# Gated heads: the value products move from the end of a slot to directly behind the scores

## What is computed

```python
def _L1_ffn_ref(x, w_q, w_k, w_gate, value_experts, output_experts):   # x already normalised
    HEADS, DIM_HEAD, EXPERTS = (8, 64, 8)
    gates = jax.nn.sigmoid((x @ w_gate).reshape(b, n, HEADS, EXPERTS).transpose(0, 2, 1, 3))
    sel = jnp.argmax(gates, axis=-1)
    gm = jax.nn.one_hot(sel, EXPERTS, dtype=x.dtype) * gates
    values = jnp.einsum('bhne,ehdk,bnd->bhnk', gm, value_experts, x)
    sim = jnp.einsum('bhid,bhjd->bhij', q * SCALE, k)
    sim = jnp.where(causal_mask, jnp.finfo(sim.dtype).min, sim)
    attn = jax.nn.softmax(sim, axis=-1)
    out = jnp.einsum('bhij,bhjk->bhik', attn, values)
    out = jnp.einsum('bhne,ehkd,bhnk->bhnd', gm, output_experts, out)
    return out.sum(axis=1)
...
    x = x + _L1_ffn_ref(_layernorm(x, axis=-1), ...)
```

## Time and profile before

| quantity | value |
|---|---|
| median of 3 runs | 3820.56 us (3817.29 to 3824.1) |
| the profiled execution, its own time | 3820.83 us |
| its span in the trace | 3819.1 us |
| PE busy (TensorE matmul) | 3505.7 us, 92% |
| DVE busy (VectorE) | 2801.9 us, 73% |
| ACT busy (ScalarE) | 2065.1 us, 54% |

### The profile page before, as it was taken

How to read it: one execution, slowest core, us unless ns; L and a number is a source line. 1 busy time by engine, 2 the same in 40 slices (tenths; PEclk the granted TensorE clock), 3 DMA queues, 4 the chain that set the end, 5 groups by cost and what they waited for, 6 DMA issues and landing times. The chain is left out here.

```text
span 3819.1 us, 91322 instructions
## 1 busy us (share of the span) xinstructions
PE 3505.7 (92%) x28322; PEld 2917.3 (76%) x28322; DVE 2801.9 (73%) x8965; ACT 2065.1 (54%) x6485; POOL 395.4 (10%) x582
## 2 busy tenths in 40 slices
PE   6999999899999999339968889999799999999999
PEld 5888888688888888239956656676588888888887
DVE  5666666677777776646658877888788878788786
ACT  5777777677777776325545548888432223222232
POOL 0000000000000000341168302222000000000000
PEclk9999999999999999669989999999899999999999
DMA  3000000010000000542211000000200000000000
GB/s 101 1 0 0 0 0 0 18 51 11 11 11 13 14 11 1 175 137 77 78 55 45 15 17 20 22 22 17 87 26 11 14 8 16 8 11 14 8 14 9
DMA packets 56108, 109.69 MB, mean 29 GB/s; under 512 B 8368, under 2 KB 27184, under 8 KB 55728
## 3 DMA queue, kind: packets, MB, share of 16 engines
q1 hardware_dynamic: 46656, 80.72, 6.7%
q0 software_dynamic: 8464, 26.22, 2.1%
q10 hardware_dynamic: 864, 1.19, 0.1%
HBM read 72.46 MB, written 35.65 MB: 28 GB/s over the span
## 5 line engine op out<-in xcount | busy, mean ns | idle before, releaser
L2255 DVE TENSOR_TENSOR f_zgT<-f_zT,f_ps_g 128x512 fp32r<-128x512 f32 x512 | 327.3, 681 | 14.0 <-PE f_ps_g L2086 9.9
L639 ACT ACTIVATE c_pr<-c_sm,c_nmx 128x256 f32<-128x256 f32 x512 | 254.5, 498 | 147.7 <-DVE c_nmx L485 147.7
L127 PE MATMUL f_ps_out<-f_out_rounded,f_zgT 128*128 128x256 f32 x1024 | 295.3, 288 | 0.0
L128 PE MATMUL f_ps_out<-f_out_rest,f_zgT 128*128 128x256 f32 x1024 | 289.5, 283 | 0.0
L2208 DVE TENSOR_TENSOR f_gv<-f_ps_v,f_gm 128x512 f32<-128x512 f32 x256 | 175.6, 686 | 154.2 <-PE f_ps_v L129 154.1
L129 PE MATMUL f_ps_out<-f_out_rounded,f_zgT 128*128 128x256 f32 x1024 | 288.0, 281 | 0.0
L639 ACT ACTIVATE a_pr<-a_sm,a_nmx 128x128 f32<-128x128 f32 (+1 forms) x512 | 227.1, 445 | 98.1 <-DVE a_nmx L485 98.1
L485 DVE CUSTOM_DVE_ANT_0 a_sm<-a_ps_s,causal 128x128 f32<-128x128 f32 (+1 forms) x512 | 152.5, 354 | 156.8 <-PE a_ps_s L371 156.7
L485 DVE CUSTOM_DVE_ANT_0 c_sm<-c_ps_s,c_mask 128x256 f32<-128x256 f32 x512 | 186.7, 420 | 87.1 <-PE c_ps_s L371 86.7
L127 PE MATMUL f_ps_v<-f_val_rounded,f_xs 128*128 128x512 f32 x512 | 214.8, 419 | 6.7 <-DVE f_gv L2208 6.7
L2337 ACT ACTIVATE f_pr<-f_sm,f_nmx 128x128 f32<-128x128 f32 (+1 forms) x256 | 115.0, 450 | 185.5 <-DVE f_nmx L2228 185.5
(11 more groups left out here) (384 smaller groups left out, 11231.8 us busy)
## 6 DMA issues: line engine op xcount, KB each, us to landing
f_slot_rows<-f_run POOLq DMA_DIRECT2D x1, 9216.0 KB, 34.8
f_rows<-f_slot_rows SPq DMA_DIRECT2D x72, 128.0 KB, 2.0
f_slot_out<-f_y SPq DMA_DIRECT2D x72, 128.0 KB, 1.9
c_ctx_stage<-in_ctxT SPq DMA_DIRECT2D x32, 256.0 KB, 2.8
small<-in_f_w SPq DMA_DIRECT2D x16, 512.0 KB, 3.9
x_sb<-in_x SPq DMA_DIRECT2D x8, 512.0 KB, 8.3
small<-in_c_w SPq DMA_DIRECT2D x8, 512.0 KB, 4.0
c_mask_stage<-in_mask SPq DMA_DIRECT2D x16, 256.0 KB, 3.0
```

The lines of the kernel that those rows point to most:

```text
L127: nc.tensor.matmul(out, sh, mh, start=start, stop=False, **kw)
L128: nc.tensor.matmul(out, sh, ml, start=False, stop=False, **kw)
L639: last = nc.scalar.activation(pr[:, r, i, 0:n], sm[:, j, i, 0:n], ACT.Exp, bias=nmx[:, j, i:i + 1], scale=-1.0, accum_out=sums[:, r, i:i + 1])
L2255: last = nc.vector.tensor_tensor(zgT[:, k % 2, r], zT[:, s % 2, r, :].bitcast(F32).unsqueeze(1).broadcast_to([P, 2, S]), ps_g[:].rearrange ...
```

## The change

The call of `values` moves, with its condition, from behind the four rounds (and behind `turn_x`) into round k = 1, directly behind `scores` and ahead of `turn`. It is the same call with the same waits inside. Nothing is changed on VectorE, ScalarE, GpSimd or the DMA queues.

```diff
@@ -2114,6 +2114,8 @@
                         project_v(now[0], s, k, b)
                     if k == 1 and ahead:
                         scores(ahead[0], ahead[1], now[0] + 1 if now else ahead[0] + 1)
+                    if k == 1 and (at := lagged(b, s, 3, STEPS)):
+                        values(at[0], at[1])
                     if k % 2 and two:
                         turn(two[0], two[1], k // 2, two[2])
                     if four:
@@ -2122,8 +2124,6 @@
                             output(four[0], four[1], k - 1, four[2])
                 if s == STEPS - 1 and (not isinstance(b, int) or b + 1 < B):
                     turn_x(b + 1)
-                if at := lagged(b, s, 3, STEPS):
-                    values(at[0], at[1])
                 if four:
                     output(four[0], four[1], K - 1, four[2])
                 if now and s == STEPS - 1:
```

## The result

The changed kernel takes 3852.84 us (median of 6 runs), the kernel before 3820.51 us in the same comparison: a ratio of 1.0082, with a 95% interval of 1.0071 to 1.0093. It is slower by 32 us; the forecast was 3852. The profiled execution of the changed kernel took 3850.67 us.

The account below looks back on a forecast made before the run. VectorE's chain from gate_v(2) to output(3) was taken as the bound, with busy TensorE merely covering its wait. Terms 29.2 + 1.65 + 2.7 - 1.9 = 31.7 us on 3820.83 gave 3852 us, range 3834 to 3868.

Parts of the forecast that it names:

- The price of the step: values between scores and turn on TensorE: delays everything behind it, project_v(2) included, by 0.80 us a slot.
- Neither bound: Limits on the cost of values at its new place: 0.47 us at least, 0.96 us at most.
- The chain from gate_v(2) to output(3): VectorE's unbroken 4.33 us from gate_v(2) to gate_z(3), whose start releases output(3) 1.32 us later; it passes on the delay.
- The slack of 0.10: VectorE's time to spare before output(3) in s = 1 and 2: 0.10 us, taken off the 0.80 us delay.
- The batch: Growth of a regular batch: 0.60 + 0.70 + 0.70 + 0.25 = 2.25 us; thirteen batches give 29.2 us.
- The end: Last batch, without turn_x, 2.7 us longer; three emptying slots gain 1.9 us as values hides in waits.
- The beginning: Batch 1 grows 1.65 us; slot 3 adds 0, and slot 4 adds 0 because its 2.11 us stall absorbs values.
- the faster one: Rival: TensorE's own stream decides, so 0.18 us a slot is gained, 3810 us; chance 6%.
- Full price: Rival: no slack counts, neither VectorE's nor turn_x; 45.3 us more, 3866 us; chance 10%.
- cheap neighbour: Rival: values costs less behind scores, 0.63 or 0.47 us, because its drain merges; 3842 or 3834 us; chance 8%.
- nothing: Rival: the delay is caught up elsewhere, as in slot 4, and time stays at 3821 us; chance 3%.
- the clock: Rival: TensorE's idle time at slot ends lowers the granted clock; some 60 us more, beyond 3900; chance 2%.

Follow-up runs that it names:

- e2: Changed kernel with VectorE's norm of the first head (0.78 us) moved from round 2 to the end of round 3: 0.9989 of the kernel before.
- e3: Changed kernel plus an unused second copy of the four products of values at the old place in s = 0, 1, 2: 1.0092 of the kernel before.
- e6: Changed kernel plus the same extra products as e3, but directly behind values at the new place, ahead of project_v(2): 1.0171 of the kernel before.
- e4: Changed kernel with e2's edit, gate_z(3) ahead of gate_v(3) on VectorE and spread_one(3) ahead of the second turn on TensorE: 0.9957 of the kernel before.
- e5: Kernel before, values at its old place, with the same cuts to VectorE's path as e4: 0.9999 of the kernel before.
- e1: Changed kernel with values in round 2, directly behind project_v(2), instead of behind scores: 1.0031 of the kernel before.
- e7: e4 without its edit on TensorE, so turn stays ahead of spread_one(3): 0.9987 of the kernel before.
- e8: e4 with scores and values in s = 1 to 3 behind spread_one(0), ahead of project_v(1): 0.9970 of the kernel before.

## Why the prediction was right, step by step

**The price of the step, 0.80 us**: right, 0.81 at the new place (3056.58 to 3057.39), with the idle times of 0.33 and 0.17 that I had taken over from the neighbours. Neither bound, 0.47 or 0.96, was near.

**The chain from gate_v(2) to output(3)**: right, 4.33 us and 1.33 us, and e2, e3 and e6 show that it is the cause. The slack of 0.10, read from a slot that truly waits, was right too: slots with s = 1 or 2 could have grown by 0.80 without it, and a batch would be 0.2 longer.

**The batch**: 2.25 us forecast, 2.26 measured between neighbouring batches. Slot by slot, from one output(3) to the next, the growth is 0.59 us in s = 0 (17.84 to 18.43), 0.69 in s = 1, 0.71 in s = 2 and 0.27 in s = 3 (17.05 to 17.32), where I had 0.60, 0.70, 0.70 and 0.25. So the parts are right, not only the sum. The 13 batches run between these additions to x_sum, before and then after (timeline of DVE):

```profile
2822.16 0.69 DVE L2263 TENSOR_TENSOR f_x_sum<-f_x_sum,f_ps_out 128x512 f32<-128x512 f32 x1 [0.97 <-PE f_ps_out L129]
...
3708.00 0.69 DVE L2263 TENSOR_TENSOR f_x_sum<-f_x_sum,f_ps_out 128x512 f32<-128x512 f32 x1 [1.08 <-PE f_ps_out L129]
```
```profile
2821.42 0.69 DVE L2263 TENSOR_TENSOR f_x_sum<-f_x_sum,f_ps_out 128x512 f32<-128x512 f32 x1 [0.43 <-PE f_ps_out L129]
...
3736.92 0.69 DVE L2263 TENSOR_TENSOR f_x_sum<-f_x_sum,f_ps_out 128x512 f32<-128x512 f32 x1 [0.54 <-PE f_ps_out L129]
```

885.84 us became 915.50: 29.7 more, where the sum had 29.2.

**The end** (last batch and emptying slots): 0.8 forecast; the last addition to x_sum starts at 3815.99 before and 3845.82 after, so from the rows above 107.99 became 108.90, 0.9.

**The beginning**: the one part that was mis-sized, by 1.3 of the 31.7 us. From the stage's first transposes (2698.56 before, 2697.50 after) to the first row above it is 123.60 before and 123.92 after: +0.3, where the sum had 1.65. Slots by the first load of project: slots 5 to 7 grew by 1.68, as forecast, and slot 3 is 12.78 us in both (the zero is right). Slot 4 is the term that failed: not zero, but 0.70 shorter (2750.80 to 2771.54 before, 2749.08 to 2769.12 after). Up to spread_one(1) it is 8.78 us in both, so values does vanish in that wait; what is gained lies behind it (last section). The remaining 0.66 us were gained in slots 0 and 1, before values runs for the first time, so the change didn't make them: in the ten traces slot 0 takes anything from 14.3 to 16.4 us, and in the kernel before it is at the top of that.

**The total**: in the profiled executions the difference is 29.8 us (29.7 + 0.9 + 0.3, less 1.1 for an earlier start of the stage); that of the medians is 32.3. The spread of single runs, 8 us for the kernel before, is wider than that gap, so the close agreement of 3852 with the median owes something to luck, and the batch is the better witness.

**What I said the profile would show**: idle time ahead of gate_v(2) of 1.3 us (measured 1.21: 0.27 and 0.94); output(3) waiting about 0.9 in s = 0, 1 and 2 (0.83 or 0.84), 0.4 in s = 3 (0.43), near 50 us in total (44.7). Scores to turn came to 1.66, as forecast (1.65).

**The rivals**: the faster one (TensorE decides) is false for this kernel, but its price was real. e4 against e5 gives 0.82 us a batch for the new place, 0.2 a slot, where I had 0.18. The rule of the Trainium skill (TensorEngine Tiling (Array Packing), Key Properties), that a change of tiling mode drains TensorE, is in line with this: one change less in a slot, and 0.2 us less. It only decides once TensorE is the bound. Full price is excluded by s = 3 (0.27 us, not 0.80), cheap neighbour by the 0.81 us of the step, nothing by the 2.26 us of every batch, and the clock by its 1.00 in the batches.

## What to carry to other kernels

An engine that is busy all the time isn't therefore the bound at every point: look for a wait of almost no idle time that recurs in nearly every round (0.2 us at most, 46 times here), for it can mark two engines that arrive together, and the step that fills the time before it is cover. A step moved forward is paid in full if it stands ahead of whatever starts the other engine's chain (0.64 to 0.80 us here) and costs far less behind it (0.1 us a slot in e3, up to 0.3 in e1); work out the slack from a place where the wait is real, slot by slot. And if a move saves work on one engine but lengthens a chain on another, keep it and shorten the chain: the two together gave 0.43%, where the move alone cost 0.82% and the chain's edits alone gave nothing.

## What the runs showed of the hardware

**The granted clock fell behind one wait, and not behind others.** In slot 4 of the kernel before, PE stands idle for 1.87 us ahead of spread_one(1) (the earlier trace rows has 2.11 on the weight side). Behind it the granted clock is 0.50, the 1.2 GHz level, from 2760 to 2762 us, and the weight loads take 0.33 us instead of 0.19. In the changed kernel values fills part of that wait, PE is idle for 1.06 us, and the clock stays at 1.00; two later waits of 0.40 and 0.77 us in the same slot don't change that. PE's timeline and the window behind the wait, before:

```profile
2759.58 0.79 PE L2086 MATMUL f_ps_g<-f_oneT,f_spread 128*128 128x256 f32 x2 [1.87 <-DVE f_zgT L2255]
```
```profile
2760.00:2763.00 3.00, 3.00 (x15) 2.94 (x15) 2.96 (x9) 0.89 (x4) 0.00 (x0) 0.54 0.01 3
```

The window of after:

```profile
2758.00:2761.00 3.00, 3.00 (x20) 2.58 (x20) 2.97 (x9) 0.62 (x3) 0.00 (x0) 1.00 0.04 14
```

The other runs repeat both pictures. e1 and e5, in which values does not stand in that wait, have 1.88 and 1.86 us of idle PE there and a granted clock of 0.50 in 2782 to 2784 and 2762 to 2764 us; e2, e3, e4, e7 and e8 have 1.05 to 1.07 us and 1.00. But the length of the wait alone does not decide it. In e6 PE is idle for 2.22 us in the same slot, ahead of the extra products, and the clock stays at 1.00:

```profile
2756.36 0.87 PE L2076 MATMUL f_ps_v<-f_prT,f_v 128*64 128x256 f32 x8 [2.22 <-DVE f_gv L2217]
```
```profile
2756.36:2759.36 3.00, 3.00 (x26) 2.69 (x27) 3.00 (x9) 1.45 (x6) 0.00 (x0) 1.00 0.03 8
```

The slower clock is a likely reason why slot 4 is longer in the kernel before. No run separates it from the other differences behind spread_one(1), so its share of the 0.70 us is only argued. The waits at output(3) in the regular batches, up to 0.84 us on the weight side, leave the clock at 1.00.

**Idle time on the weight side isn't a price.** Ahead of scores it read 0.36 us, and moving scores away from the wide products gained nothing (e8). In the row of values from e5 none is printed, and 0.21 us were lost there. What counts is from start to start over the whole stretch.
